# Mixture-of-experts rows scattered by expert, read and returned as plain blocks, in a macaron block on one core

## The reference, cut to what matters

```python
x = x + 0.5 * ffn(layernorm(x))
x = x + deltanet(layernorm(x))
x = x + 0.5 * ffn(layernorm(x))
```

```python
weights, indices = top_k(softmax(xf @ gate_w.T), 2)
weights = weights / weights.sum(-1)
out  = sum over the two:  weight * (silu(xf @ w_gate[e]) * (xf @ w_up[e])) @ w_down[e]
out += sigmoid(xf @ shgate_w) * ((silu(xf @ shw_gate) * (xf @ shw_up)) @ shw_down)
```

## Time and profile before

| | us |
|---|---|
| median of three runs | 1254.88 |
| lowest and highest | 1252.7 and 1256.25 |
| span of the profiled execution | 1247.3 |
| PE busy in the span | 1013.0 (81%) |
| DVE busy | 791.5 (63%) |
| POOL busy | 659.9 (53%) |
| ACT busy | 478.9 (38%) |

### The profile page before, as it was taken

How to read it: one execution, slowest core, us unless ns; L and a number is a source line. 1 busy time by engine, 2 the same in 40 slices (tenths; PEclk the granted TensorE clock), 3 DMA queues, 4 the chain that set the end, 5 groups by cost and what they waited for, 6 DMA issues and landing times.

```text
span 1247.3 us, 22940 instructions
## 1 busy us (share of the span) xinstructions
PE 1013.0 (81%) x6928; PEld 923.9 (74%) x6928; DVE 791.5 (63%) x2299; ACT 478.9 (38%) x1303; POOL 659.9 (53%) x758
## 2 busy tenths in 40 slices
PE   2745978499999659999999999977756899996674
PEld 2745877489999538888888888777745799995674
DVE  4335756356676557888888865545653567664675
ACT  3223332145555324445445544222321355552111
POOL 3646656244443445667767735245663444443884
PEclk9866889689999868899999989778857899998877
DMA  7584435034434210000000001055660244342433
GB/s 224 30 136 68 20 18 18 5 109 124 123 120 111 64 37 20 27 27 24 29 27 27 18 2 35 1 18 21 31 35 3 86 123 124 119 122 77 141 102 119
DMA packets 63733, 79.92 MB, mean 64 GB/s; under 512 B 12352, under 2 KB 54816, under 8 KB 63616
## 3 DMA queue, kind: packets, MB, share of 16 engines
q1 hardware_dynamic: 46336, 42.83, 20.0%
q0 software_dynamic: 17280, 35.62, 11.4%
HBM read 46.88 MB, written 31.52 MB: 63 GB/s over the span
## 4 chain that ended last, share of the span: by engine, by line
PE 50%; POOL 14%; DVE 11%; issue 10%; DMA 7%; DVEq 2%; ACT 2%; another core or an unknown queue 1%; SPq 0%; POOLq 0%; ACTq 0%
PE PSA L1447 13%; PE PSA L1548 7%; POOL MEM L897 5%; PE PSA L1499 4%; POOL tokens L846 4%; PE PSA L1465 4%; POOL MEMR L862 3%; PE PSA L1430 3%; PE PSA L1455 3%; PE PSA L1374 2%; DMA tokens<-CN,POSU 2%; DVEq L1076 2%; DVE X L1274 2%; PE PSA L1403 2%; PE PSA L1519 2%
## 5 line engine op out<-in xcount | busy, mean ns | idle before, releaser
L876 POOL DMA_INDIRECT MEM<-normed,SLOT x142 | 134.9, 950 | 164.1 <-PE PSA L1430 156.6
L1388 PE MATMUL PSA<-MEMR,SGUh 128*128 128x256 f32 (+1 forms) x768 | 185.5, 325 | 8.8 <-DVE MEM L1164 6.2
L1447 PE MATMUL PSA<-EGUh,MEMR 128*128 x568 | 177.0, 353 | 3.5 <-issue 2.0
L1403 PE MATMUL PSA<-SDh,MEMR 128*128 128x256 f32 (+1 forms) x384 | 105.9, 339 | 78.3 <-POOL MEMR L862 71.2
L897 POOL DMA_INDIRECT MEM<-expert_out,POSU x128 | 124.4, 972 | 53.8 <-issue 28.7
L1388 PEld LDWEIGHTS PSA<-MEMR,SGUh 128*128 128x128 f32 (+1 forms) x768 | 147.6, 221 | 6.9 <-DVE MEM L1164 6.4
L846 POOL DMA_INDIRECT tokens<-CN,POSU x128 | 124.7, 974 | 43.9 <-issue 32.1
L1403 PEld LDWEIGHTS PSA<-SDh,MEMR 128*128 128x128 f32 (+1 forms) x384 | 82.7, 239 | 83.5 <-POOL MEMR L862 58.9
L976 ACT ACTIVATE MEM<-PSA 128x256 f32<-128x256 f32 (+1 forms) x96 | 36.5, 380 | 245.0 <-POOL MEMR L862 136.1
L1548 PEld LDWEIGHTS PSA<-MEM 128*128 128x128 f32 x1024 | 125.7, 199 | 1.5 <-DVE MEM L1324 1.5
L1548 PE MATMUL PSA<-MEM 128*128 128x18 f32 x1024 | 124.6, 265 | 1.1 <-DVE MEM L1324 1.1
(11 more groups left out here) (174 smaller groups left out, 2584.9 us busy)
## 6 DMA issues: line engine op xcount, KB each, us to landing
expert_out<-MEM SPq DMA_DIRECT2D x142, 128.0 KB, 1.7
normed<-MEM SPq DMA_DIRECT2D x16, 512.0 KB
X<-in_L_attn_x SPq DMA_DIRECT2D x8, 512.0 KB, 7.7
out<-X SPq DMA_DIRECT2D x8, 512.0 KB, 4.1
MEM<-normed,SLOT POOLq DMA_INDIRECT x142
tokens<-CN,POSU POOLq DMA_INDIRECT x128
MEM<-expert_out,POSU POOLq DMA_INDIRECT x128, 2.8
MEM<-in_L_ffn_w_gate SPq DMA_DIRECT2D x8, 176.0 KB, 8.2
```

What stands on the lines that cost most here:

```text
L876: pool.indirect_dma_start(out=XG[j % 4], out_offset=None, in_=xn_d[f], in_offset=bass.IndirectOffsetOnAxis(ap=SLOT[:, j:j + 1], axis=0)).t ...
L1388: last = mm(t[0:h, w * HALF:(w + 1) * HALF], SGU[b][:, w, k, j * P:j * P + h], XT[slot][a][:, k, hf * HALF:(hf + 1) * HALF], start=i == 0, ...
L1403: last = mm(t[:, c * D:(c + 1) * D], (HH, HL)[a][m % 3][0:h, c * P:(c + 1) * P], SD[b][0:h, j, :], start=j == 0 and i == 0 and c == 0, sto ...
L1447: last = mm(t[:, 0:2 * HE], XGR[j % 2][a][:, k, :], EGU[b][:, bass.ds(e, 1), k, :], start=i == 0, stop=i == 3 * KD - 1)
```

## The change

It has four parts.

1. **Rows by expert.** `normed` and `tokens` go. The array `expert_rows` has 8 regions of 4096+128 rows (ES) and 7 more blocks of 128, each row 258 floats (RW): the 256 normalised values, the token's first expert, and twice its number. POOL scatters the rows themselves from XN to their two places (64 scatters for each f, of 1032 bytes a row instead of 4), and XN is free again only when those have landed. After the last of them POOL clears a filler block, and SP writes 15 blocks of filler rows for each f: 7 behind the regions, 8 at the end of what each expert holds, at addresses read from the counts NEI.
2. **Blocks.** A slot is then a plain block of 128 rows: SP reads its address from SRC and loads it (71 for each f). POOL computes from the row's two extra values where its result belongs (L884 of the new kernel, 128x1) and scatters y there (L889), so that the two results of a token lie side by side in `expert_out`. A tile's results are one block of 128 by 2 KB, loaded by SP with one transfer (32 for each f). The steps `lines` and `where` go.
3. **Batches side by side.** A group holds the same position of the 4 batches, so chunk n is batch n%4. The state goes from chunk n-4 to chunk n, in place in 4 buffers.
4. **SiLU in one.** ACT computes SiLU from the PSUM product, and the DVE operations L1162 (96) and L1252 (142) go. The router's weights come from a tanh instead of an exponential, with a few DVE operations less.

Parts of the difference:

```diff
             def scatter(r, c):
                 n = norms[r]
+                i = n.g * GT + c
                 for k in range(2):
-                    pool.indirect_dma_start(out=id_d[n.f], out_offset=bass.IndirectOffsetOnAxis(ap=POSU[:, k, i:i + 1], axis=0),
-                                            in_=tok[:, i:i + 1], in_offset=None).then_inc(s_sct, 16)
+                    pool.indirect_dma_start(out=rows_d[n.f], out_offset=bass.IndirectOffsetOnAxis(ap=POSU[:, k, i:i + 1], axis=0),
+                                            in_=XN[n.xn][:, c, :], in_offset=None).then_inc(s_xst[n.xn], 16)
...
+            def slots(f):
+                sp.wait_ge(s_blank, f + 1)
+                for w in range(E - 1):
+                    sp.dma_start(rows_d[f][E * ES + w * P:E * ES + (w + 1) * P, :], FILL[:, E + w:E + w + RW]).then_inc(s_fill, 16)
+                sp.wait_ge(s_ends, f + 1)
+                ends = [sp.value_load(NEI[0:1, e:e + 1], min_val=e * ES, max_val=e * ES + ROWS) for e in range(E)]
+                for e, end in enumerate(ends):
+                    sp.dma_start(rows_d[f][bass.ds(end, P), :], FILL[:, e:e + RW]).then_inc(s_fill, 16)
...
+                row = sp.value_load(SRC[0:1, j:j + 1], min_val=0, max_val=E * ES + (E - 2) * P)
+                sp.dma_start(XG[j % 4], rows_d[f][bass.ds(row, P), :]).then_inc(s_fetch[j % 4], 16)
...
+                sp.dma_start((YG1, YG2)[f][i % ring], y_view[f][:, i, :]).then_inc(s_yg[f][i % ring], 16)
...
+            def expert_down(f, j):
+                taken(pool, ("y", f, j))
+                pool.wait_ge(s_yidx, f * SLOTS + j + 1)
+                pool.indirect_dma_start(out=y_d[f], out_offset=bass.IndirectOffsetOnAxis(ap=YIDX[:, j % 8:j % 8 + 1], axis=0),
+                                        in_=YS[j % 3], in_offset=None).then_inc(s_ys[j % 3], 16)
...
-                a(TH[m % 2][0:h, :], t[0:h, 0:HALF], ACT.Tanh, scale=0.5).then_inc(s_th, 1)
+                a(TH[m % 2][0:h, :], t[0:h, 0:HALF], ACT.Silu).then_inc(s_th, 1)
...
-                v.scalar_tensor_tensor(TH[m % 2][0:h, :], TH[m % 2][0:h, :], 1.0, t[0:h, 0:HALF], ALU.add, ALU.mult)
-                settle()
                 v.tensor_tensor(TH[m % 2][0:h, :], t[0:h, HALF:2 * HALF], TH[m % 2][0:h, :], ALU.mult).then_inc(free(("gu", f, g, hf, j)), 1)
```

More of the change, by code:

```diff
@@ L215, in table @@
         self.add("slots", f)
-        for s in between[1:5]:
-            s()
-        self.take(("lines", f))
-        self.add("lines", f)
-        for s in between[5:]:
+        for s in between[1:]:
             s()
@@ L229, in experts @@
             self.add("fetch", f, j)
-        self.add("where", f)
         self.xg(f, 0)
@@ L532, in build @@
         part = zone(ZN, ZH)
-        XN = [part(GT * D).rearrange("p (c d) -> p c d", c=GT) for _ in range(3)]
+        XN = [part(GT * RW).rearrange("p (c d) -> p c d", c=GT) for _ in range(3)]
         part = zone(ZH, ZT)
@@ L571, in build @@
         VA = [part(HEADS * VW).rearrange("p (h d) -> p h d", d=VW) for _ in range(3)]
-        YG1 = [[part(D) for _ in range(2)] for _ in range(2)]
+        YG1 = [part(2 * D) for _ in range(2)]
         part = zone(ZT, ZT + 1536)
@@ L584, in build @@
         part = zone(ZH, ZT)
-        U = [part(16 * VW).rearrange("p (a n) -> p a n", a=2) for _ in range(2)]
+        U = [part(16 * VW).rearrange("p (a n) -> p a n", a=2) for _ in range(B)]
         DS = part(16 * VW).rearrange("p (a n) -> p a n", a=2)
@@ L715, in low_engine, with stored, f_end, routed @@
             return "dve" if k in DVE_PIECES or pieces[k][1][i][3] is ER else "pool"
+        def stored(r, k):
+            return 128 * sum(n.kind == "F" and n.xn == k for n in norms[:r])
+        first_unit = min(i for i, k in enumerate(units) if k[1] == 1)
+        def f_end(f):
+            return 1 + max(i for i, n in enumerate(norms) if n.kind == "F" and n.f == f)
+        norm_a = {n.g: i for i, n in enumerate(norms) if n.kind == "A"}
+        def routed(r):
+            return sum(n.kind == "F" for n in norms[:r])
+        def lows(engine, m):
+            return plan.low[:m].count(engine)
+        def low_done(eng, m):
+            eng.wait_ge(s_hl if plan.low[m] == "pool" else s_hv, lows(plan.low[m], m) + 1)
+        def y_stores(f, k):
+            per = len(range(k, SLOTS, 3))
+            return 16 * per * (f + 1)
         @block.sync
         def _(sp):
-            sp.dma_start(X[:, 0:GT, :], xt_view[:, 0:GT, :]).then_inc(s_x[0], 16)
+            sp.dma_start(X[:, 0:GT, :], x_view[:, 0]).then_inc(s_x[0], 16)
             sp.dma_start(CN[:, 0:C_FIRST], c_d[:, 0:C_FIRST]).then_inc(s_const, 16)
-            sp.wait_ge(s_zero, 1)
-            for f in range(2):
-                sp.dma_start(id_d[f].rearrange("(p n) a -> p (n a)", p=P), BLANK).then_inc(s_blank, 16)
             def load(k):
@@ new lines, in collect @@
+            def collect(f, i):
+                if i == 0 and f == 1:
+                    for k in range(3):
+                        sp.wait_ge(s_ys[k], y_stores(1, k))
+                if i == 0 and f == 0:
+                    for k in range(3):
+                        sp.wait_ge(s_ys[k], y_stores(0, k))
+                ring = len(s_yg[f])
+                if i >= ring:
+                    sp.wait_ge(s_cmb, NT * f + i - ring + 1)
+                sp.dma_start((YG1, YG2)[f][i % ring], y_view[f][:, i, :]).then_inc(s_yg[f][i % ring], 16)
@@ L762, in store @@
             def store(g):
                 sp.wait_ge(s_out, g + 1)
-                sp.dma_start(ot_view[:, g * GT:(g + 1) * GT, :], X[:, g * GT:(g + 1) * GT, :]).then_inc(s_store, 16)
-            run(plan, {"load": load, "scale": scale, "expert_down": expert_down, "store": store})
+                sp.dma_start(o_view[:, g], X[:, g * GT:(g + 1) * GT, :]).then_inc(s_store, 16)
+            run(plan, {"load": load, "slots": slots, "fetch": fetch, "collect": collect, "store": store})
             sp.wait_ge(s_store, 16 * NG)
-        def stored(r, k):
-            return 16 * sum(n.kind == "F" and n.xn == k for n in norms[:r])
@@ L773, in build @@
-        placed = 16 * 2 * NT
-        first_unit = min(i for i, k in enumerate(units) if k[1] == 1)
-        def f_end(f):
-            return 1 + max(i for i, n in enumerate(norms) if n.kind == "F" and n.f == f)
-        norm_a = {n.g: i for i, n in enumerate(norms) if n.kind == "A"}
-        def routed(r):
-            return sum(n.kind == "F" for n in norms[:r])
-        def lows(engine, m):
-            return plan.low[:m].count(engine)
-        def low_done(eng, m):
-            eng.wait_ge(s_hl if plan.low[m] == "pool" else s_hv, lows(plan.low[m], m) + 1)
@@ L792, in states @@
-        def states(n):
-            return n - n // CB
-        def y_stores(f, k):
-            per = len(range(k, SLOTS, 3))
-            return 16 * per * (f + 1)
         @block.gpsimd
```

263 lines of the change are left out of this document (110 added, 153 removed).

## The result

The changed kernel takes 1125.09 us in the median of four runs (1123.98 to 1125.44), against 1255.57 of the kernel before beside it; the ratio on record is 0.902 with a 95% interval of 0.8945 to 0.9095 (the two medians divided give 0.896, inside it). The forecast was 1161, with a range of 1130 to 1205: the sign was right and none of the rivals A to D occurred, the gain was 130 us instead of 94, and the median lies 5 us under the range's lower end. The profiled execution has a span of 1123.5 us, 123.8 less than before.

The account below looks back on a forecast made before the run. No one engine bound the whole: PE the experts and mid-attention, POOL's order the last stage and feed. Terms −26 −11 −24 −6 −4 −25 −2 +4 = −94 gave span 1153, time 1161, range 1130 to 1205.

Parts of the forecast that it names:

- rivals A to D: A: jam stays, 1198, 0.15; B: scatters bind feed, 1267, 0.09; C: last stage unshortened, 1186, 0.13; D: experts stretch, 1204, 0.05.
- the feed of f=1: Stage before the second experts: gain 11 us (0 to 20), two waits for an unknown queue read as DMA congestion.

Follow-up runs that it names:

- the second profile of the same kernel: Changed kernel with the batches one behind the other again, run once more: attention stretch 353.0 us against 339.6 in its first profile; median 1130.73, unaltered 1131.07.

## What to carry to other kernels

Before calling an engine a bound, ask whether its busy time was measured at a low clock or has its ends modelled: the first falls when the waits go (67.7 us at 0.80, 51.0 at 0.96), the second can hide waits of some 0.15 us, which 142 slots turn into 22 us. Where an engine's time to issue list-addressed transfers binds, as here, the gain of making them a plain block by scattering once on the way in lies first in the issue (0.55 us for a block against 2 x 1.22 for two gathers) and only then in the engine that issues. And one profile that agrees with a theory is not enough where the granted clock takes part: the second profile of the same kernel took the proof away. The same goes for a forecast that comes true: the feed of f=1 hit its number in one trace, and the next eleven did not bear out its reason.

## What was not expected of the hardware

A read of one number from memory into a register of PE takes 300 ns in the median in most kernels here and 415 to 418 in two of them (340 in f=0 of one of these), with the slot longer by about 0.1 us. The attention stretch took 340 or 353 us in two executions of one kernel, at mean granted clocks of 0.91 and 0.87, and 349 to 358 in all but two of the traces. A switch of ACT's tables cost its load of 1.28 us and 0.02 us on each side of it. A packet of a 1 KB row store held its engine for 0.83 us beside 4-byte scatters in one kernel, and for 0.05 us beside 4-byte and row scatters in another.
